# A fused patch-token, attention and expert block: the softmax maximum subtracted on VectorE, 64-row score products, values split by upper halves

## What is computed

```python
h = concatenate([tokens(x), txt], axis=1)            # 64 x 113 x 128
q, k, v = layernorm(h) @ Wq, @ Wkv                   # 8 heads of 64
scores = einsum('bqhd,bkhd->bhqk', q * 0.125, k).astype(bfloat16)
probs = softmax(scores, axis=-1)
out = einsum('bhqk,bkhd->bqhd', probs.astype(float32), v).astype(bfloat16)
h = h + out @ Wo + bo
x = layernorm(h)
h = h + shared_expert(x) + sum over the 3 best of 16 experts of gating * expert(x)
```

## Time and profile before

| | |
|---|---|
| median of three runs | 974.72 us (974.15 to 976.13) |
| the profiled execution | 971.3 us, of which the span from first to last instruction is 969.5 us |
| PE busy in the span | 699.7 us |
| DVE busy | 632.5 us |
| ACT busy | 461.0 us |
| POOL busy | 681.4 us |
| TensorE clock granted, mean | 0.899 of 2.4 GHz |

### The profile page before, as it was taken

One profiled execution on the slowest core, in us unless ns is written; L12 is line 12 of the kernel. 1 busy time (PEld: TensorE's weight loads), 2 busy tenths in 40 slices (PEclk: granted clock), 3 DMA queues, 4 the chain that ended last, 5 costly groups with the idle time before them and its releaser, 6 DMA issues.

```text
span 969.5 us, 20598 instructions
## 1 busy us (share of the span) xinstructions
PE 699.7 (72%) x5680; PEld 582.5 (60%) x5680; DVE 632.5 (65%) x1723; ACT 461.0 (48%) x1091; POOL 681.4 (70%) x784
## 2 busy tenths in 40 slices
PE   4473499887997879878788787689877777776000
PEld 3362388776776768767677676458665655655000
DVE  1198478898999988999899788534333333333186
ACT  2021388776877867767677564114332323332000
POOL 4169444588787887878788778746777777777553
PEclk9686699999999999999999898589999999999555
DMA  8540000000000000000000000166665665663196
GB/s 200 157 136 22 12 1 2 9 26 28 19 27 19 22 29 17 27 22 22 27 17 24 20 24 27 40 184 200 202 183 170 178 183 168 176 186 111 50 347 215
DMA packets 71471, 85.57 MB, mean 88 GB/s; under 512 B 13943, under 2 KB 65152, under 8 KB 71355
## 3 DMA queue, kind: packets, MB, share of 16 engines
...
...
## 4 chain that ended last, share of the span: by engine, by line
POOL 32%; issue 31%; PE 11%; DMA 6%; DVE 5%; POOLq 2%; ACT 1%; SPq 0%; DVEq 0%
POOL dispatched L528 11%; POOL expert_rows L541 8%; POOL s L483 7%; DMA x2t<-expert_rows 3%; POOL h L489 2%; DMA expert_rows<-yb,kz 2%; POOL rs L495 2%; PE bank L729 2%; PE bank L598 2%; PE bank L778 2%; DVE h L1258 1%; POOL ve L493 1%; PE bank L682 1%; PE bank L712 1%; PE bank L787 1%
## 5 line engine op out<-in xcount | busy, mean ns | idle before, releaser
L541 POOL DMA_INDIRECT expert_rows<-yb,kz x200 | 194.4, 972 | 75.4 <-issue 55.4
L528 POOL DMA_INDIRECT dispatched<-pay,sloti x192 | 198.7, 1035 | 60.9 <-issue 60.1
L483 POOL TENSOR_TENSOR s<-s,mx 113x904 bf16<-113x904 bf16 x64 | 109.4, 1709 | 49.9 <-DVE mx L1139 49.3
L1246 DVE TENSOR_TENSOR yb<-bank,kz 128x256 f32<-128x256 f32 x100 | 42.4, 424 | 142.8 <-DMA expert_rows<-yb,kz 139.2
L729 PE MATMUL bank<-kz,qt 128*113 128x226 f32 x512 | 112.1, 363 | 0.3 <-ACT kz L859 0.3
L778 PE MATMUL bank<-xe,w_ex 128*128 128x256 f32 x400 | 105.8, 388 | 0.0
L917 ACT ACTIVATE xe<-bank 128x256 f32<-128x256 f32 x100 | 38.3, 383 | 139.7 <-PE bank L766 132.1
L598 PE MATMUL bank<-xt,wqkv 128*128 128x452 f32 x384 | 103.2, 400 | 0.9 <-DVE xt L1157 0.7
L787 PE MATMUL bank<-w_ex,hide 128*128 128x128 f32 x400 | 67.6, 292 | 48.6 <-DVE hide L1236 46.4
L787 PEld LDWEIGHTS bank<-w_ex,hide 128*128 128x128 f32 x400 | 55.5, 192 | 75.1 <-DVE hide L1236 58.8
L729 PEld LDWEIGHTS bank<-kz,qt 128*113 128x113 f32 x512 | 89.6, 185 | 6.8 <-issue 0.7
...
## 6 DMA issues: line engine op xcount, KB each, us to landing
w_ex<-in_w_ffn ACTq DMA_DIRECT2D x100, 192.0 KB, 2.5
kz<-dispatched SPq DMA_DIRECT2D x100, 130.0 KB, 2.4
...
dispatched<-pay,sloti POOLq DMA_INDIRECT x192, 2.3
...
```

The lines of the kernel that those rows point to most:

```text
L483: nc.gpsimd.tensor_tensor(s16[k % 2][0:T, :, :], s16[k % 2][0:T, :, :], mx[k % 2][0:T, :].unsqueeze(2).to_broadcast([T, H, T]), ALU.subtra ...
L528: pool.indirect_dma_start(out=xs_dram[:, :], out_offset=bass.IndirectOffsetOnAxis(ap=sloti[:, b // GRP, b % GRP, c:c + 1], axis=0), in_=pa ...
L541: pool.indirect_dma_start(out=y_dram[:, :], out_offset=bass.IndirectOffsetOnAxis(ap=xs[slot][:, j, ROW - 1:ROW].bitcast(I32), axis=0), in_ ...
```

## The change

Five things are done.

- The subtraction of the maximum goes from POOL to DVE, right behind the maximum, with a wait on it. For this `s16` becomes `[128, T, H]`, head innermost, so that the eight maxima are read as they lie, again and again. ACT writes the scores with a step of eight elements, the maximum and the exponential read with it.
- The copy of the transposed probabilities goes from DVE to ACT, in the place that the copy L849 had.
- The keys lie in `kt` as they come, with one copy instruction of 128 partitions in place of two of 64 into `kz`. A head's scores are a product over 64 partitions: eight matmuls of 113 columns in place of four of 226, even heads in bank 3, odd heads in bank 4. The two zero fills are gone.
- The values are split by bits. `vf` and `vr` hold fp32, and the bf16 part of each is the upper half of every word, read with a step of two elements (`top_half`). ACT's copy L849 is gone; DVE subtracts twice.
- `w_ex` lies over `kt`; `xs` and `tab` have a tensor of their own.

```diff
-        kz = [sb(f"kz{i}", [128, NC, GRP, 2, T]) for i in range(2)]
-        v1 = [sb(f"v1_{i}", [128, H, DH + 1], BF16) for i in range(4)]
-        v23 = [sb(f"v23_{i}", [128, 2, H * DH], BF16) for i in range(4)]
-        s16 = [sb(f"s16_{i}", [128, H, T], BF16) for i in range(2)]
+        kt = [sb(f"kt{i}", [128, NC, GT]) for i in range(2)]
+        vf = [sb(f"vf{i}", [128, H, DH + 1]) for i in range(4)]
+        vr = [sb(f"vr{i}", [128, H, DH]) for i in range(4)]
+        v3 = [sb(f"v3_{i}", [128, H, DH], BF16) for i in range(4)]
+        def top_half(a):
+            return a.bitcast(BF16)[:, :, 1::2]
+        v1 = [top_half(vf[i][0:T, :, :]) for i in range(4)]
+        v2 = [top_half(vr[i][0:T, :, :]) for i in range(4)]
+        s16 = [sb(f"s16_{i}", [128, T, H], BF16) for i in range(2)]
...
-            for i in range(2):
-                nc.gpsimd.memset(kz[i][:, :, :, :, :].rearrange("p c b e t -> p (c b e t)"), 0.0).then_inc(S["kz_zero"], 1)
...
-                    after(pool, "max_done", n)
-                    nc.gpsimd.tensor_tensor(s16[k % 2][0:T, :, :], s16[k % 2][0:T, :, :],
-                                            mx[k % 2][0:T, :].unsqueeze(2).to_broadcast([T, H, T]), ALU.subtract).then_inc(S["sub_done"], 1)
...
-                        for j in range(2):
-                            m = nc.tensor.matmul(dst[:, at:at + DH], probs, v23[(k - 1) % 4][0:T, j, hh * DH:(hh + 1) * DH],
+                        nc.tensor.matmul(dst[:, at:at + DH], probs, v2[(k - 1) % 4][:, hh, :], start=False, stop=False)
+                        m = nc.tensor.matmul(dst[:, at:at + DH], probs, v3[(k - 1) % 4][0:T, hh, :], start=False, stop=True)
...
                     for c in range(NC):
-                        m = nc.tensor.matmul(bank[3 + c // 2][0:T, (c % 2) * 2 * T:(c % 2 + 1) * 2 * T],
-                                             qt[gs][:, c, ks * T:(ks + 1) * T],
-                                             kz[gs][:, c, ks, :, :].rearrange("p e t -> p (e t)"), start=True, stop=True)
+                        for e in range(2):
+                            half_p = slice(e * DH, (e + 1) * DH)
+                            m = nc.tensor.matmul(bank[3 + e][0:T, c * T:(c + 1) * T], qt[gs][half_p, c, ks * T:(ks + 1) * T],
+                                                 kt[gs][half_p, c, ks * T:(ks + 1) * T], start=True, stop=True)
...
-                if ok(n):
-                    after(act, "vr_done", n)
-                    nc.scalar.activation(v23[k % 4][0:T, 0, :], vr[k % 2][0:T, :], ACT.Copy).then_inc(S["v2_done"], 1)
+                if ok(n - 1):
+                    after(act, "pt_done", n - 1)
+                    nc.scalar.activation(pt[(k - 1) % 2][0:T, :, 0:TP],
+                                         bank[5][0:T, :].bitcast(BF16).rearrange("p (h t) -> p h t", h=H)[:, :, 0:TP],
+                                         ACT.Copy).then_inc(S["pt_copied"], 1)
...
-                    for e in range(2):
-                        half_p = slice(e * DH, (e + 1) * DH)
-                        m = nc.scalar.activation(kz[1 - g][half_p, kk, :, e, :],
-                                                 bank[2][half_p, 0:GT].rearrange("p (b t) -> p b t", b=GRP), ACT.Copy)
+                    nc.scalar.activation(kt[1 - g][:, kk, :], bank[2][:, 0:GT], ACT.Copy).then_inc(S["k_copied"], 1)
...
-                    nc.scalar.activation(p16[k % 2][0:T, :, :], s16[k % 2][0:T, :, :], ACT.Exp).then_inc(S["exp_done"], 1)
+                    nc.scalar.activation(p16[k % 2][0:T, :, :], s16[k % 2][0:T, :, :].rearrange("p t h -> p h t"), ACT.Exp).then_inc(S["exp_done"], 1)
...
-                        m = nc.scalar.activation(s16[(k + 1) % 2][0:T, 4 * i:4 * i + 4, :].rearrange("p h t -> p (h t)"),
-                                                 bank[3 + i][0:T, 0:4 * T], ACT.Copy)
+                        m = nc.scalar.activation(s16[(k + 1) % 2][0:T, :, i:H:2].rearrange("p t c -> p c t"), bank[3 + i][0:T, 0:4 * T].rearrange("p (c t) -> p c t", t=T),
+                                                 ACT.Copy)
...
-                    nc.vector.reduce_max(mx[i][0:T, :], s16[i][0:T, :, :], AX.X).then_inc(S["max_done"], 1)
+                    nc.vector.reduce_max(mx[i][0:T, :], s16[i][0:T, :, :].rearrange("p t h -> p h t"), AX.X).then_inc(S["max_done"], 1)
+                    after_all(dve, ("txt_in", 16), ("max_done", n, 1))
+                    nc.vector.tensor_tensor(s16[i][0:T, :, :], s16[i][0:T, :, :],
+                                            mx[i][0:T, :].unsqueeze(1).to_broadcast([T, T, H]), ALU.subtract).then_inc(S["sub_done"], 1)
                 routing(o, k, 0)
-                if ok(n - 1):
-                    after(dve, "pt_done", n - 1)
-                    nc.vector.tensor_copy(pt[1 - i][0:T, :, 0:TP],
...
-                    after(dve, "v2_done", n)
-                    nc.vector.tensor_tensor(v23[k % 4][0:T, 1, :], vr[i][0:T, :], v23[k % 4][0:T, 0, :], ALU.subtract).then_inc(S["v_ready"], 1)
+                    after_all(dve, ("txt_in", 16), ("vr_done", n, 1))
+                    nc.vector.tensor_tensor(v3[k % 4][0:T, :, :], vr[k % 4][0:T, :, :], v2[k % 4], ALU.subtract).then_inc(S["v_ready"], 1)
```

31 lines of the change are left out of this document (12 added, 19 removed).

## The result

The changed kernel takes 1222.24 us, median of four runs (1217.41 to 1222.6), beside 974.67 for the kernel before: a ratio of 1.254 (1.250 to 1.259). The forecast was 928 us, range 904 to 964, so it has the wrong sign. The profiled execution takes 1222.6 us with a span of 1220.8.

The account below looks back on a forecast made before the run. Behind octet 0 POOL set the pace at 7.79 us a step, DVE close behind. With DVE the bound at 6.9, 55 steps save 49 us, octet 0 loses 2: 971.3 profiled becomes 924, forecast 928 us, range 904 to 964.

Parts of the forecast that it names:

- The strided maximum: DVE's maximum over head-innermost scores: no extra cost for the stride, staying at 1.09 us.
- the present 0.54 and 0.957 us: ACT's strided score copies and strided exponential: priced at their present times, 0.54 and 0.957 us.
- Rival 1: Scattered 16-bit accesses cost ACT: 937 to 968 us, chance 0.17 for shrunken gain; 0.11 for slower, 980 to 1060.
- the slower part: Part of Rival 1 where ACT's surcharge, from about 1.07 times the slope, makes the kernel slower: 980 to 1060, chance 0.11.
- the subtraction at 0.62: Subtraction of the maximum on DVE, all operands dense 16-bit: 0.62 us a step, with 1.09 kept as other end.
- rival 4: DVE's subtraction goes one element at a time, 1.09 us: 7.37 us a step, 954 us; chance 0.10.
- the copy of the probabilities at 0.91: Copy of the transposed probabilities, 912 elements, moved to ACT: 0.91 us a step.
- L1185 back from 1.00 to L1179's 0.675: DVE's rest of the values, delayed behind POOL's subtraction: falls from 1.002 to 0.675 us.
- the additions behind the subtraction: DVE's additions of 64 elements lose their delay behind POOL's subtraction: 1.041 to 0.207 us each.
- POOL no longer the bound: POOL loses the 1.71 us subtraction: 44.4 us an octet, 5.6 a step, narrowly leaving the bound.
- the scores at 1.6 us: PE's sixteen score passes of 113 columns: 1.6 us a step, with ends of 0.8 and 3.2.
- Rival 3: PE's array halves work side by side, scores take 0.8 us: 6.75 us a step, 914 us; chance 0.12.

Follow-up runs that it names:

- The probe: Kernel before with some thirty single instructions behind its end, each alone on its engine, measuring strided accesses on ACT and DVE; its time is not used.
- e12: Changed kernel, same layout, but ACT's two score copies go position by position through four heads instead of head by head: 986.71 us, ratio 1.015.
- e1: Changed kernel with s16 as before, each head in one piece; subtraction stays on DVE, one element at a time: 939.54 us, ratio 0.967.
- f10: e6 with padded keys, score products of 226 columns, two key copies and zero fills, run side by side with f6: 919.37 us, ratio 0.946.
- f6: e6 run again, side by side with f1 and f10: 901.39 us, ratio 0.927.
- e6: e1 with DVE subtracting in pairs, maxima doubled by ACT, and the subtraction later, behind the next norm's statistics: 900.49 us, ratio 0.925.
- f1: e1 run again, side by side with f6 and f10: 943.43 us, ratio 0.969.

## Why the prediction was wrong, step by step

- **The step that failed** is the layout, in two places. "The strided maximum I price at nothing: L1046 reads 192 elements with a step of 64 bytes in 0.363 us", and for ScalarE "I take the present 0.54 and 0.957 us, the nearest rows". L1046 does step 64 bytes, but it comes back to each 16-byte piece after three accesses. The probe's L1316, back after twelve, already pays the full surcharge, and L1308, with one element from each piece, takes 1.75 against 1.09. The row stood for another access pattern. And the rows for ScalarE's write were no rows of a strided write at all: measured are 2.365 us for 0.539, and 1.844 for 0.957.
- **Rival 1 had the mechanism and the path, and the wrong size.** It asked for a surcharge of 1.07 times the slope on each element to turn the sign, and went up to twice. Measured: (2.365 - 0.539) / 452 = 0.0040 us for a write, five times the 0.00081; (1.844 - 0.957) / 904 = 0.0010 for the exponential's read, 1.2 times. Its own sum then gives 6.34 + 2 x 1.83 + (0.89 - 0.33) = 10.56 us a step, against 11.45 measured. With the 0.69 of the maximum it would be 11.25, but the chain passes the maximum in 10 of 59 steps only, so that agreement would be luck. What is left, 0.9 us, holds the maximum of those steps and PE's slower passes (a clock of 0.80 for 0.97, L681 at 0.338 us where L682 before took 0.268). How it divides was not separated; in e12 the copies are shorter by 2 x 1.68 = 3.36 us and the step by 11.45 - 7.74 = 3.71. The 0.11 for the slower part (980 to 1060) was too little and its range too short: nothing in the trace of before bore on ScalarE's strided writes, for or against, and the row of L1046 did not show what it was set against the page for.
- **The Trainium skill's rule** on lines of 16 bytes ("Advanced Engine Details and Errata", Memory Cachelines), weighed there against one row, was right for this layout. The trace agrees with 2.365, 1.844 and 1.778 us.
- **Right:** the subtraction at 0.62 (0.630 measured; the other end, 1.09, is the by-head form at 1.10, so rival 4 is what e1 runs), though the reason given overlooks that L1139, 1.086 us, is itself a 16-bit operation with all of it in SBUF; the copy of the probabilities at 0.91 (0.943); L1185 back from 1.00 to L1179's 0.675 (0.698); the additions behind the subtraction; POOL no longer the bound.
- **Mis-sized:** the scores at 1.6 us take 0.98. Rival 3 had the mechanism (0.8). While DVE sets the pace, as the forecast had it, this should be worth little; that was not run. f10 against f6 says 18 us, with the key copies, once DVE is faster.
- **The pace without the layout.** The forecast of 6.9 us a step and 928 us put a subtraction of 0.62 beside copies of 0.54. No run with this layout has both: e12 comes nearest, with copies of 0.687, and keeps the long exponential and maximum. e6 has both, by pairs and with the subtraction in another place, and takes 900.5 us (6.44 a step in f6). Take e1, which is rival 4 nearly to the letter (a subtraction of 1.09, a layout that costs nothing), 954 was its price and 939.5 the measurement: 7.09 us a step in f1 against 7.37. DVE's busy time for eight steps was 57.47 x 8 x 7.09 / 61 = 53.4 us there, where the rival had 52.8 + 3.8 = 56.6; which of its terms was too long is open.
